# A two-layer graph network on one core: setup cut into pieces, tiles placed by halves of 128 bytes, one product of the layer norm on GpSimd, and four engine queues in a new order

## What is computed

```python
# layer 0, for each graph: two graph attentions, layer norm, feed-forward with relu, layer norm
Wh = h @ W;  e = leaky_relu(Wh @ a[:F] + (Wh @ a[F:]).T)
h  = softmax(where(adj > 0, e, -9e15), axis=1) @ Wh            # twice: W1, a1, then W2, a2
h  = layernorm(x + h);  y = layernorm(h + relu(h @ w_ff1 + b_ff1) @ w_ff2 + b_ff2)
# layer 1: 8 heads; v is chosen by the edge's kind r = 0..3
attn = softmax(q @ k.T / sqrt(32))
out  = sum_r (attn * (adj == r)) @ (y @ Wv[r] + bv[r])
x    = layernorm(y + out @ Wo + bo);  out = layernorm(x + gelu(x @ W1 + b1) @ W2 + b2)
```

## Time and profile before

| | us |
|---|---|
| median of three runs | 3175.42 |
| lowest and highest | 3172.79, 3175.61 |
| the profiled execution | 3170.61 |
| its span in the trace | 3168.7 |
| PE busy | 3073.1 (97% of the span) |
| ACT busy | 2429.1 (77%) |
| DVE busy | 2314.9 (73%) |
| POOL busy | 1759.8 (56%) |

### The profile page before, as it was taken

How to read it: one execution, slowest core, us unless ns; L and a number is a source line. 1 busy time by engine, 2 the same in 40 slices (tenths; PEclk the granted TensorE clock), 3 DMA queues, 4 the chain that set the end, 5 groups by cost and what they waited for, 6 DMA issues and landing times.

```text
span 3168.7 us, 78187 instructions
## 1 busy us (share of the span) xinstructions
PE 3073.1 (97%) x26980; PEld 2760.4 (87%) x26980; DVE 2314.9 (73%) x4978; ACT 2429.1 (77%) x6218; POOL 1759.8 (56%) x1485
## 2 busy tenths in 40 slices
PE   4899999999999999999999999999999999999996
PEld 3789889889889889889889889889889889889885
DVE  5677777777777777777777777777777777777763
ACT  2677787787787787787787787787787787787774
POOL 1455565565565565565565565565565565565553
PEclk7999999999999999999999999999999999999998
DMA  5000100100100100100100100100100100100100
GB/s 135 28 25 24 33 26 23 33 26 23 33 26 23 33 26 23 33 26 23 33 26 23 33 26 23 33 26 23 33 26 23 33 26 23 33 26 23 33 12 14
DMA packets 108072, 93.55 MB, mean 30 GB/s; under 512 B 19072, under 2 KB 107264, under 8 KB 108032
## 3 DMA queue, kind: packets, MB, share of 16 engines
q1 hardware_dynamic: 108032, 93.01, 9.8%
HBM read 76.17 MB, written 16.78 MB: 29 GB/s over the span
## 4 chain that ended last, share of the span: by engine, by line
PE 73%; issue 10%; POOL 8%; ACT 4%; DVE 3%; SPq 1%; POOLq 1%; DMA 0%; DVEq 0%; ACTq 0%
PE ps_f L257 8%; PE ps_f L258 7%; PE ps_f L259 7%; PE ps L257 5%; PE ps L258 5%; PE ps L259 5%; PE ps L422 4%; PE ps_ao L442 4%; PE ps_ao L485 4%; PE ps L432 4%; PE ps_g L257 3%; POOL res L962 3%; PE ps_g L258 3%; PE ps_g L259 3%; POOL norm L962 3%
## 5 line engine op out<-in xcount | busy, mean ns | idle before, releaser
L970 POOL TENSOR_TENSOR hid_lo<-hid_full,hid_hi 128x512 fp32r<-128x512 f32 x512 | 764.9, 1494 | 533.6 <-ACT hid_hi L599 522.8
L257 PE MATMUL ps_f<-down_w_hi,hid_hi 128*128 128x256 f32 x2048 | 589.2, 288 | 2.1 <-POOL hid_lo L970 1.9
L258 PE MATMUL ps_f<-down_w_lo,hid_hi 128*128 128x256 f32 x2048 | 572.8, 280 | 0.0
L259 PE MATMUL ps_f<-down_w_hi,hid_lo 128*128 128x256 f32 x2048 | 572.2, 279 | 0.0
L822 DVE TENSOR_REDUCE s_least<-ps 128x4 f32<-128x1024 f32 x256 | 310.8, 1214 | 295.2 <-PE ps L422 295.2
L614 ACT ACTIVATE prob<-ps,s_least 128x256 f32<-128x256 f32 x1024 | 470.6, 497 | 4.9 <-DVE s_least L822 3.8
L953 POOL TENSOR_TENSOR rstd<-vareps,neg_half 128x2 f32<-128x2 f32 x256 | 178.4, 697 | 462.0 <-DVE vareps L770 462.0
L831 DVE SCALAR_TENSOR_TENSOR masked<-adj_in,prob 128x1024 f32<-128x1024 int32 x256 | 386.6, 1530 | 40.1 <-ACT prob L622 40.1
L257 PEld LDWEIGHTS ps_f<-down_w_hi,hid_hi 128*128 128x128 f32 x2048 | 385.8, 188 | 32.0 <-issue 25.0
L258 PEld LDWEIGHTS ps_f<-down_w_lo,hid_hi 128*128 128x128 f32 x2048 | 386.6, 189 | 2.3
L259 PEld LDWEIGHTS ps_f<-down_w_hi,hid_lo 128*128 128x128 f32 x2048 | 386.8, 189 | 0.0
(11 more groups left out here) (157 smaller groups left out, 9377.0 us busy)
## 6 DMA issues: line engine op xcount, KB each, us to landing
adj_in<-adj_keys SPq DMA_DIRECT2D x128, 256.0 KB, 2.8
xT_in<-x_features SPq DMA_DIRECT2D x64, 256.0 KB, 2.7
norm<-x_nodes SPq DMA_DIRECT2D x64, 256.0 KB, 2.7
out_nodes<-norm SPq DMA_DIRECT2D x64, 256.0 KB, 2.1
raw_up<-L_w_ff SPq DMA_DIRECT2D x1, 1024.0 KB, 5.2
raw_down<-L_w_ff SPq DMA_DIRECT2D x1, 1024.0 KB, 7.9
raw_v<-L_Wv SPq DMA_DIRECT2D x4, 256.0 KB, 7.8
raw_up<-L_W SPq DMA_DIRECT2D x1, 1024.0 KB, 9.2
```

Source lines behind the costliest of these rows:

```text
L257: nc.tensor.matmul(ps_out, left[0], right[0], start=first, stop=False)
L258: nc.tensor.matmul(ps_out, left[0], right[1], start=False, stop=False)
L259: return nc.tensor.matmul(ps_out, left[1], right[0], start=False, stop=last)
L970: pool.tensor_tensor(hid[1][:, 2 * m:2 * m + 2, :], hid_full[:, 2 * m:2 * m + 2, :], value(hid[0][:, 2 * m:2 * m + 2, :]), ALU.subtract).t ...
```

## The change

1. **Layout.** Weights are given out in another order, `gat_w` and `wh` get 288 columns instead of 260 and 258, and three spacers of 64 bytes (`half_row`) are put in. By the shapes, left and right now start modulo 128 at: up, q and k, down, first attention and mixing 0 and 64, v 64 and 0. Down was there already.
2. **Norm.** `dve_norm` gets a sixth instruction that writes the negative mean (`below`), `dve_norm_end` goes, and `pool_rstd` multiplies `below` by `rstd` on POOL.
3. **Order.** The four lists of a pass are written anew.
4. **Setup.** Vectors come from two arrays that the host joins, in four DMAs in place of about thirty; the order of the loads changes; the splits are cut into pieces that stand at several places of the passes -3 to -1; each first use has a wait of its own.
5. `dve_adj_top` writes to a tile of its own.

```diff
+        ROW, HALF = 32, 16
+        WIDE = -(-WX // ROW) * ROW
+        def half_row(n):
+            return sb(f"half_row{n}", [P, HALF])
...
+        half_row(0)
+        gat_w = tuple(t[:, :, 0:WX] for t in pair("gat_w", [P, C, WIDE]))
...
-        def dve_norm_end(dve, g, n):
...
+            dve.tensor_reduce(below[n][:], meanvar[n][:, :, 0:1], AX.X, ALU.add, negate=True).then_inc(below_set[n].sem, 1)
...
             pool.tensor_tensor(rstd[n][:], vareps[n][:], neg_half[:], ALU.pow).then_inc(rstd_set[n].sem, 1)
+            pool.wait_ge(*rstd_set[n](g, 1))
+            pool.wait_ge(*below_set[n](g, 1))
+            pool.tensor_tensor(centre[n][:], below[n][:], rstd[n][:], ALU.mult).then_inc(centre_set[n].sem, 1)
...
         def pool_body(pool, t, nxt, gat, ff0, att1, ff1):
-            if att1:
-                pool_affine(pool, b, 2)
-            if gat:
-                pool_rstd(pool, c, 1)
-            if ff0:
-                pool_rec_wide(pool, a, 1)
+            if gat:
+                pool_rstd(pool, c, 1)
+            if ff0:
+                pool_rec_wide(pool, a, 1)
+            if att1:
+                pool_affine(pool, b, 2)
...
+            sp.dma_start(raw_a[:], across(vectors[15 * D:19 * D])).then_inc(gat_in.sem, 16)
+            sp_features(sp, 0)
+            sp_edges0(sp, 0)
+            sp.dma_start(col_vectors[:], columns).then_inc(columns_in.sem, 16)
+            sp.dma_start(raw_up[0][:], rows(p0["w_ff1"])).then_inc(up_in[0].sem, 16)
+            sp.dma_start(raw_down[0][:], rows(p0["w_ff2"])).then_inc(down_in[0].sem, 16)
+            sp_nodes(sp, 0)
+            sp.dma_start(row_vectors[:], across(vectors[0:12 * D])).then_inc(vectors_in.sem, 16)
...
-            gat_ready(eng)
             body(eng, -3, True, False, False, False, False)
-            if setup:
-                setup(eng)
             body(eng, -2, True, True, False, False, False)
-            ready(eng)
```

More of the change, by code:

```diff
@@ L14, in __call__, with adj_seq_kernel @@
         return self.sem, g * self.per_graph + n
-def adj_seq_kernel(nc: bass.Bass, x, xT, adjT, p0, p1, out):
+def adj_seq_kernel(nc: bass.Bass, x, xT, adjT, p0, p1, vectors, columns, out):
     f32, f32r, i32 = mybir.dt.float32, mybir.dt.float32r, mybir.dt.int32
@@ L124, in adj_seq_kernel @@
         att_s, score = staged_pair("att_s", "score", [P, C, N])
-        wh = pair("wh", [P, C, WE])
+        half_row(2)
+        wh = tuple(t[:, :, 0:WE] for t in pair("wh", [P, C, WIDE]))
+        hT = [pair(f"hT{n}", [P, C, N]) for n in range(3)]
         wh12 = sb("wh12", [P, C, 2])
@@ L138, in adj_seq_kernel @@
         rstd = [sb(f"rstd{n}", [P, C]) for n in range(4)]
-        hT = [pair(f"hT{n}", [P, C, N]) for n in range(3)]
+        below = [sb(f"below{n}", [P, C]) for n in range(4)]
         adj1_in = sb("adj1_in", [P, C, N], i32)
+        adj_rest = sb("adj_rest", [P, C * N])
+        neg_half = sb("neg_half", [P, C])
         adj_top, adj_reaches = sb("adj_top", [P, 1]), sb("adj_reaches", [P, 1])
@@ L328, in adj_seq_kernel, with first @@
                    [ps1[:, 0, :], ps1[:, 1, :], ps_f[:, 0, :], ps1[:, 0, :]]]
+        def first(g):
+            return isinstance(g, int) and g == 0
         def pe_up(pe, g, l, m):
+            if first(g) and m == 0:
+                pe.wait_ge(up_biased[l].sem, 1)
             if m == 0:
@@ L354, in pe_down @@
         def pe_down(pe, g, l, i, half):
+            if first(g) and i == 0 and half == 0:
+                pe.wait_ge(down_lo_made[l].sem, 4)
             if i == 0 and half == 0:
@@ L411, in pe_scores @@
         def pe_scores(pe, g, hg):
+            if first(g) and hg == 0:
+                pe.wait_ge(up_biased[1].sem, 1)
             if hg == 0:
@@ L592, in act_hidden @@
         def act_hidden(act, g, l, m):
+            if first(g) and l == 0 and m == 0:
+                act.wait_ge(down_lo_made[0].sem, 4)
             act.wait_ge(*up_done[l](g, m + 1))
@@ L608, in act_prob @@
         def act_prob(act, g, hg, m):
+            if first(g) and hg == 1 and m == 0:
+                act.wait_ge(down_lo_made[1].sem, 4)
             for h in (2 * m, 2 * m + 1):
@@ new lines, in pe_up_setup, with dve_bias_setup @@
+        def pe_up_setup(pe, l):
+            pe.wait_ge(columns_in.sem, 16)
+            pe.wait_ge(up_in[l].sem, 16)
+            for u in range(UC):
+                for k in range(C):
+                    last = nc.tensor.matmul(ps1[:, 2 + l, u:u + 1], raw_up[l][:, k, nodes(u)],
+                                            shift_col[ff_in[l]][:, k:k + 1], start=(k == 0), stop=(k == C - 1))
+            last.then_inc(up_shifted[l].sem, 1)
+        def dve_bias_setup(dve, l):
+            dve.wait_ge(up_lo_made[l].sem, C)
+            dve.wait_ge(up_shifted[l].sem, 1)
+            dve.tensor_tensor(up_bias[l], up_bias[l], ps1[:, 2 + l, 0:UC], ALU.add).then_inc(up_biased[l].sem, 1)
```

549 lines of the change are left out of this document (273 added, 276 removed).

## The result

Four runs of the changed kernel took 3145.30 to 3154.32 us, median 3150.56; the kernel before, run beside it, 3174.57. The ratio is 0.9927, 95% interval 0.9915 to 0.9939: 0.7% faster, where 3155 was forecast. The profiled execution took 3147.39 us (forecast 3151), with a span of 3145.6.

The account below looks back on a forecast made before the run. The prediction took PE's work in each of 61 passes, its waits and the setup to bound the kernel. Passes were to give 0 and setup -20 us, so 3175.4 - 20 = 3155 us, range 8 in 10 from 3105 to 3203.

Parts of the forecast that it names:

- Layout, 0.8 us a pass: PE's up, q, k and attention products: new start addresses make them faster, 0.8 us a pass, the middle of 0.28 and 1.30.
- if all go at 113: Upper bound of the layout gain: up, q, k, attention and half of down at 113 ns a matmul, 1.30 us a pass.
- The rival that the layout gives nothing: Up, q, k and attention products: no gain from addresses, up stays at 120 ns, total 3200 us; chance 0.18.
- What goes, -0.37: Two PE waits vanish each pass: 0.20 us ahead of norm 1's transposes, 0.17 in the second half of the turns.
- Changes of kind, -0.20: Heads group 1 on PE, now one piece: fewer switches between narrow and full-width products save 0.20 us a pass.
- v, +1.0: PE ahead of v's second half: a new wait of 1.0 us every pass for DVE's eviction of v.
- D + 3.4: Forecast end of DVE's eviction of v, 3.4 us after D, the start of wh1 behind down 0's last half.
- Norm 2, +0.3: PE at up(a,0,1): waits 0.3 us a pass until DVE's norm 2 has read `ps_ao`.
- The loop's sum, 0: All terms of one pass together: -0.07 us, rounded to 0, so the 61 passes give nothing.
- Norm on GpSimd, 0: The norm's extra product on POOL: off PE's path, 0 in the loop and at most half a us at the end.
- Setup, -20: Time ahead of the passes: second mixing 27 us earlier, 7 given back later, so 20 us less, between 26 and 12.
- My own sign of being wrong: Wrong if the first output product starts above 145 us, or the 61 passes' length changes by more than 50 us.

Follow-up runs that it names:

- e1: The changed kernel with its tiles put back to the old places, order and setup as changed: 3170.49 us, ratio to before 0.9985.
- e2: The kernel before with nothing but the new layout of the tiles: 3145.61 us, ratio to before 0.9917.
- e6: Probe without the network: TensorE alone runs blocks of 36 matmuls at the kernel's own tile distances and varied places; 64 and 0 took 4.18 us, 0 and 0 4.40.
- e8: The changed kernel with the four lists of a pass in the order of before: 3139.82 us, ratio to before 0.9897.
- e9: The changed kernel with the places of loaded and streamed operands swapped (64 and 0; v 0 and 64): 3130.52 us, ratio to before 0.9859.
- e4: Probe without the network: TensorE alone runs blocks with tiles of 520 columns at varied places; 0 and 64 took 117.5 to 118.1 ns, 64 and 0 120.1 to 121.4.
- e12: Probe without the network: TensorE alone runs up products at four pairs of places behind eleven kinds of work; 64 and 0 took 113.3 ns in 14 of 22 blocks.
- e11: The changed kernel without its three 64-byte spacers, so every operand starts at 0 modulo 128: 3170.58 us.

## Why the prediction was right in its total and not in its terms

- **Bound.** Right: PE is busy for 2895 of 2937 us, and passes, setup and draining account for 23.1 of the 23.2 us by which the profiled execution is shorter.
- **Layout, 0.8 us a pass.** The mechanism is right, the term mis-sized by two: 0.38 (e1) to 0.48 (e2). By classes of the table: up 96 x 4.1, q and k 24 x 2.2, attention 36 x 0.9, less down 96 x 1.2 and v 12 x 3.1, 0.33. The step that failed is "if all go at 113": I took the mean of two bounds, where down, already in its place, lost its fast blocks, and q and k never got them. v, left out for want of a row, lost a little. The larger part of the losses of v and of down is there in e1 too (233.6 and 117.3), at the old places, and so belongs to the order. The rival that the layout gives nothing fell with e1 and e2. The Trainium skill ("SBUF — State Buffer", section "Who interferes with whom") calls PE's two read ports independent and lets only the port pair shared by VectorE and GpSimd contend. The trace does not agree with a layout term of 0, which I had drawn from that rule: addresses alone move the pace by up to 6.7 ns in 120, with every other engine idle (e6). Whether the read ports are what they act on, no run shows.
- **What goes, -0.37.** Measured -0.39: the piece from the products with v to the transposes of norm 1 went from 1.23 to 0.98 us, and the second half of the turns from 1.01 to 0.87.
- **Changes of kind, -0.20.** Heads group 1 with wh1 went from 2.62 to 2.39; some 0.1 of it comes back at up(d,1,1), which now stands right behind products with v.
- **v, +1.0.** Right in place, name and frequency, 0.75 in size: of D + 3.4 the eviction took 0.2 less, as `below`, the reciprocal and it overlap by more than I counted, and PE arrived 0.1 later.
- **Norm 2, +0.3.** 0.15: the half of the turns ahead of up(a,0,1) takes 0.95 us where eight transposes without a wait take 0.79. The forecast row of up(a,0,1) with an idle time and `norm` named did not come.
- **Not in the sum.** The output product waited 0.11 a pass for `ao` before and no longer does (8 matmuls in 1.83 us, now 1.72). I had the hint in the second of the earlier trace rows and did not follow it. The first attention's products in one block instead of two: -0.10; v behind narrow products: +0.10.
- **The loop's sum, 0.** -0.25. The terms above sum to about -0.1; the rest is spread over first matmuls of blocks and I did not resolve it. My layout was 0.4 too good, and the waits 0.4 too bad.
- **Norm on GpSimd, 0.** The chain from `vareps` to `centre` took 2.06 to 2.87 us before and 1.05 to 1.84 now, a larger gain than I looked for. At norm 1, the only one that PE waited for, it went from 2.06 to 1.38, and that is the order (POOL's affine steps of norm 2 moved behind it): in e8, with the norm on POOL but the old order, it is 2.09. So 0 stands for the part alone.
- **Setup, -20.** -4.2. This is the term that failed by most. My own sign of being wrong, a first output product above 145, came true: it starts at 150.74, and at 145.4 to 152.6 in all kernels with this setup. The chain to the second mixing was about right (24.7 in this execution, up to 30 in others, for 27), what comes back was not: 7 forecast, 20.6 measured. I had named the wait for the splits (about 5, measured 6.8) and the bias products, but I let the wait overlap with others, did not price the lower clock behind it, and did not follow the new order through the passes in which its cover is missing, though the earlier trace rows showed such a pass.
- **Draining, 0.** -4.0. About 0.9 of it are 8 transposes that moved from behind the last output products to ahead of the first. With the old places 3.6 of it remain (e1), with the old order 1.8 (e8), so the order has the larger part; not taken apart further.

The forecast held by luck: two errors of about 15 us, the setup's and the loop's, had opposite signs. The range, 3105 to 3203, said how little the terms were known; the chain of reasons was worth less than the hit suggests.

## What to carry to other kernels

Where a loop is bound by float32r matmuls on TensorE, look at start-to-start times of blocks of one shape: if they differ at the same granted clock, try the start addresses of what is loaded and what is streamed against each other; equal starts modulo 128 bytes were slow here, 64 for the loaded and 0 for the streamed the best (e9, 20 us below the change and 1.4% below the kernel before, by six 64-byte spacers). With the shorter tiles of e4 it was the other way round, 64 and 0 at 120 and more, so the pair is not to be carried over without a measurement. Measure such a layout in the kernel, since the order picks among the paces that a place allows. And before a step is moved, list who waits for it on every engine, third ones too, and look at the passes of filling, in which the steps that cover it are left out.

## What the runs showed of the hardware that I had not expected

- A float32r block of 256 columns at full clock runs most often at one of three paces, 113.3, 117.8 or 120.0 ns, in the network and with all other engines idle (e6, e12); other places in e6 gave 116.7 to 119.1. In e12 0 and 0 and 64 and 64 took 120.0 to 120.3 in all 44 blocks, 0 and 64 and 64 and 0 took 113.3 or 117.8 from block to block.
- Places modulo 128 are not the whole rule: with shorter tiles 64 and 64 took 117.7 (e4), with all at 0 the kernel's blocks took 118.4 to 118.8 (e11), and 0 and 96 took 120.0 (e6).
- One-column matmuls count as busy in the profile and yet the granted clock fell behind them, here and in e11 (from 71.77, the clock at 0.50 from 77 to 79): from 76.69 to 80.18 PE did 32 of them, and from 81.3 on, busy all the while, the down products ran at 213 ns and half clock for 3.3 us (window 80 to 85: clock 0.66 with PE busy for 5.00).
